# Four reorderings in a software-pipelined transformer-and-grid kernel: attention bias sum on GpSimd in slot 14, derivative sum ahead of a score, adapter copy ahead of a tanh, norm of x2 ahead of x4's scaling

## The chip, the core and the metric

One core of one Trainium2 chip runs the whole program. The metric is the device time of one execution in microseconds, the median of several. The engines are named as the profile names them: PE (TensorE matmul), PEld (its weight loads), DVE (VectorE), ACT (ScalarE), POOL (GpSimd) and SP (SyncE, which here only issues DMAs).

## What is computed

For each of 16 samples of 256 x 256 numbers, four stages follow each other. Cut to what matters here:

```python
# L0: adapter with a per-sample expert, then a norm
hidden = gelu(x @ down_W.T + down_b)
hidden = hidden @ expert_W[id].T + expert_b[id] + domain_emb[id]
x = layernorm(hidden @ up_W.T + up_b + x) * gamma + beta
# L1: adaptive norm, attention of 16 heads with a bias and a mask, feed-forward
x1 = _ln(x) * (1 + scale) + shift
scores = q @ k.T / 4 + attention_bias; scores = where(mask, -inf, scores)
x2 = x1 + (softmax(scores) @ v) @ Wo + bo
x3 = x2 + gelu2(_ln(x2) * g2 + beta2 @ W1 + b1) @ W2 + b2      # gelu2(u) = u*sigmoid(1.702u)
# L2: one of three small networks by the sample's kind, then a norm
x4 = x3 + net(x3);  f = layernorm(x4) * gamma + beta
# L3: finite differences on a grid
df = -(d/dx(A0 f) + d/dy(A1 f)) + 0.5 * (second differences of B f)
out = maximum(f + df * dt, 0)
```

## The kernel before

Everything is laid out by hand. A loop over **turns** t = -2 to 18 is unrolled; each turn has 16 **slots** s = 0 to 15, one for each attention head. In a turn six samples are at work at once, in six phases: G (sample t+2: the adapter of L0), F (t+1: norm, x1, and the projections q, k, v), X (t: the scores of its 16 heads, one a slot), B (t-1: end of attention, x2, its norm n3, first half of the feed-forward), T (t-2: second half of the feed-forward, x3, the small network, x4, its norm f, and the products of f with the grids), U (t-3: the derivatives and the output). Each engine has its own program, written slot by slot in a fixed order; semaphores tie them together, and an engine that waits for one lets everything behind it wait.

What matters around the change:

- **POOL** (lines 443 to 491) has in each turn, in this order: the reciprocal square root of the variance of y (`power`, L449), x3c = x3 + bc (L466, slot 4), x1res = x1 + bo (L472, slot 5), the mask of F (L475, slot 6), `power` for x4 (slot 7), `power` for x2 (slot 8), x2b = x2 + b2 (L484, slot 13), `power` for xa (slot 13) and bcf (L489, slot 15). x1res has two buffers, by the sample's parity. So the x1res of F may be written only when B, which uses the same buffer, has made its x2: that is the wait for `x2_ready`, which DVE sets in slot 8 (L894).
- **DVE** (lines 824 to 955): at the head of each slot the score's bias and row maximum (L826, two instructions for the two halves of the rows, "bias s" below). Behind it come, among others: w = derivative sum + t_e (L851, slot 4), x2 and its statistics (L894, L753 to L760, slot 8), scaling of x4 (`norm_scale`, L773), norm of x2 (`norm_apply`, L766, gives n3) and shift of x4 (`norm_shift`, L781, gives f) in slot 9, n3l (L905) in slot 10, the grid products of f (L810), the feed-forward's product (L922) in slots 12 to 15. In the profile's rows x4, x3, x2 and x1 are all printed as `x`, n3 and ctxN as `n`, and the grids' products t_a, t_b as `wb`, t_c as `x`.
- **ACT**: the exponentials (L526), most copies of turned scores (L512), in slots 11 to 14 the first feed-forward layer (L594) and its tanh (L599), and in slot 12 the adapter copy g1 (L602), which stands behind the tanh.
- **PE**: in slot 4 the turning of x1 into `front_bank` (L975), which first waits for `w_ready`, since w is read from that bank; in slot 5 the first layer of the small network (L1005, `back_bank<-ctxT,wb`), with weights that SP loads in each turn (`wb`, L402); in slot 10 the turning of n3 (L975, `attend_bank<-ident,n`); in slot 13 the adapter's last product (L1244), which waits for g1.
- **SP**: in slot 0 it loads a pair of bias tiles, for which it waits until DVE has done bias 15 of the turn before (L358), then issues 16 small DMAs that stack the second half of q and k for the scores (L371, L372), and in slot 1 the load of `wb` (L402).

Of the kernel before, what the change touches and what calls it, by code (L numbers as in the profile page):

```python
# [7 lines left out]
ALU = mybir.AluOpType  # L8
# [88 lines left out]
def build(nc, d):  # L97

    with ExitStack() as ctx:
# [325 lines left out]
        def _(e):  # L425
# [28 lines left out]
            def body(t):  # L454
                G, F, X, B, T, U = phases(t)
                for s in range(SLOTS):
# [6 lines left out]
                    if s == 4 and T:  # L463
                        e.wait_ge(ev["bcf_ready"], T.n)
                        e.wait_ge(ev["x3_turned"], T.n)
                        e.tensor_tensor(x3c[:, :, :], x3[:, :, :], rows(bcf[:, :]), ALU.add).then_inc(ev["x3c_ready"], 1)  # L466
                    if s == 5 and F:
                        wait(e, ev["x2_ready"], F.i - 1)
                        e.wait_ge(ev["x1_turned"], F.n)
                        if t == -1:  # L470
                            e.wait_ge(ready, 3 + SET0)
                        e.tensor_tensor(x1res[:, F.par, :, :], x1[:, :, :], rows(bo[:, :]), ALU.add).then_inc(ev["x1res_ready"], 1)  # L472
# [22 lines left out]
        def _(e):  # L495
# [18 lines left out]
            def body(t):  # L514
# [3 lines left out]
                for s in range(SLOTS):  # L518
# [71 lines left out]
                    if s in (11, 12, 13, 14) and B:  # L590
                        j = s - 11
                        quarter(e, "w1_done", B, j)
                        for m in range(2 * j, 2 * j + 2):
                            i = e.activation(ffT[:, m, :], two((bbank, abank)[j % 2])[:, m % 2, :], ACT.Identity, bias=b1c[:, m:m + 1])  # L594
                        i.then_inc(ev["u1_ready"], 1)
                        quarter(e, "u1_ready", B, j)
                        if j >= 2:
                            quarter(e, "ff_ready", B, j - 2)
                        e.activation(th[:, j % 2, :, :], ffT[:, 2 * j:2 * j + 2, :], ACT.Tanh, scale=0.851).then_inc(ev["th_ready"], 1)  # L599
                    if s == 12 and G:  # L600
                        e.wait_ge(ev["expert_done"], G.n)
                        e.activation(g1[:, :], fbank[:, 0:S], ACT.Identity, bias=wexp[:, A:A + 1]).then_inc(ev["g1_ready"], 1)  # L602

# [8 lines left out]
        def _(e):  # L612
# [199 lines left out]
            def body(t):  # L812
                G, F, X, B, T, U = phases(t)
                for s in range(SLOTS):
                    for t0, s0, setup in ((-2, 5, set_projections), (-1, 9, set_feed_forward), (0, 3, set_conditional),
                                          (0, 5, set_grids), (0, 8, set_edges)):
                        if is_step(t, s, t0, s0):
                            setup()
                    if X:
                        head(e, scored, X, s)  # L820
# [26 lines left out]
                    if s == 4 and U:  # L847
                        e.wait_ge(ev["d_done"], U.n)
                        e.wait_ge(ev["e_ready"], U.n)
                        e.wait_ge(ev["e_cols"], U.n)  # L850
                        e.tensor_tensor(t_e[:, :, :], two(fbank), t_e[:, :, :], ALU.add).then_inc(ev["w_ready"], 1)  # L851
                        e.wait_ge(ev["w_ready"], U.n)
                        e.scalar_tensor_tensor(out=t_e[:, :, :], in0=t_e[:, :, :], scalar=dt[:, bass.ds(U.i, 1)], in1=fN[:, :, :],
                                               op0=ALU.mult, op1=ALU.add).then_inc(ev["w2s_ready"], 1)
# [36 lines left out]
                    if s == 8 and B:  # L891
# [3 lines left out]
                        e.wait_ge(ev["x2_ready"], B.n)  # L895
                        norm_stats(B, 2, x2, ev["x2_stats"], ev["x2_aggr"], ev["x2_var"])
                    if s == 9 and T:
                        norm_scale(T, 3, x4, gamma3[:, :], ev["x4_rstd"], ev["f_scaled"])
                    if s == 9 and B:
                        norm_apply(B, 2, n3, x2, ev["x2_rstd"], ev["n3_ready"])  # L900
                    if s == 9 and T:
# [417 lines left out]
```

## Time and profile before

| | |
|---|---|
| median of 3 runs | 966.0 us (964.74 to 970.55) |
| the profiled execution | 969.76 us, of which the span of the trace is 967.6 us |
| mean granted PE clock over the span | 0.984 of full speed |
| PE busy | 853.4 us, 88% |
| PEld busy | 717.6 us, 74% |
| DVE busy | 730.9 us, 76% |
| ACT busy | 608.8 us, 63% |
| POOL busy | 164.1 us, 17% |
| DMA | 137.57 MB, mean 142 GB/s |

The span has three parts. Up to about 180 us the pipeline fills, from there to about 868 us each turn has the same work, and then it drains. A busy share is a mean over all three. In the timelines a row is one instruction, or several alike merged (x4), with its start, its length, and in square brackets the idle time of its engine just before it and what ended that. An instruction's start and length include the time in which it waits for a memory port.

### The profile page before, as it was taken

To read this page: it belongs to the slowest core of one execution; us is meant where nothing else is said; L and a number is where in the kernel's file an instruction comes from. 1 tells how busy PE (TensorE), PEld (TensorE's weight loads), DVE (VectorE), ACT (ScalarE), POOL (GpSimd) and SP (SyncE) were. 2 spreads that over 40 slices of the span, in tenths; PEclk is the share of its full clock that TensorE was granted. 3 is DMA by queue.
4 is the path that set the end of the run, shared out by engine and by line. 5 is a ranking of instruction groups with operands and counts; after the bars stand their busy time and mean duration, and the time that the engine had idled before them with its cause. 6 is when DMAs were issued, how large, how long until landed. Compare 5 with 4: busy or idle time off the path is not lost.

```text
span 967.6 us, 18458 instructions
## 1 busy us (share of the span) xinstructions
PE 853.4 (88%) x5962; PEld 717.6 (74%) x5962; DVE 730.9 (76%) x2441; ACT 608.8 (63%) x1247; POOL 164.1 (17%) x160
## 2 busy tenths in 40 slices
PE   2486789999999999999999999999999999898974
PEld 0274668788878878888888888887887888787773
DVE  3538676797878789696979787887979697859465
ACT  1113668786767676776868676767777686667420
POOL 2011002030211211210302112112102030211010
PEclk9997999999999999999999999999999999999988
DMA  6614365546453645555454635454544545362100
GB/s 205 199 50 128 129 184 170 153 140 175 135 175 104 180 138 162 156 159 161 141 174 153 165 118 160 138 167 151 168 153 148 170 145 165 108 172 91 47 26 22
DMA packets 147735, 137.57 MB, mean 142 GB/s; under 512 B 19298, under 2 KB 144803, under 8 KB 147636
## 3 DMA queue, kind: packets, MB, share of 16 engines
q1 hardware_dynamic: 147636, 136.33, 47.4%
q8 instruction: 53, 0.87, 0.4%
q14 instruction: 46, 0.38, 0.1%
HBM read 98.49 MB, written 4.23 MB: 106 GB/s over the span
## 4 chain that ended last, share of the span: by engine, by line
PE 57%; ACT 13%; DVE 13%; POOL 5%; SPq 5%; issue 5%; DMA 2%; POOLq 0%; DVEq 0%; ACTq 0%
PE back_bank L1034 10%; PE turn_bank L990 7%; PE front_bank L1059 5%; PE front_bank L1028 5%; PE context_bank L1044 5%; PE score_bank L1092 4%; PE score_bank L1093 4%; PE back_bank L1005 3%; PE back_bank L1014 3%; ACT sc L526 3%; PE attend_bank L1014 3%; PE attend_bank L1028 2%; ACT ffT L594 2%; POOL mask_neg L475 2%; SPq L306 2%
## 5 line engine op out<-in xcount | busy, mean ns | idle before, releaser
L826 DVE CUSTOM_DVE_ANT_0 sc<-score_bank,side 128x256 f32<-128x256 f32 x512 | 195.4, 419 | 92.3 <-PE score_bank L1093 84.7
L526 ACT ACTIVATE sc<-sc,negmax 128x256 f32<-128x256 f32 x512 | 230.0, 499 | 25.4 <-DVE negmax L826 24.9
L512 ACT ACTIVATE pt<-turn_bank 128x512 f32<-128x512 f32 x176 | 104.7, 595 | 176.0 <-PE turn_bank L990 144.8
L990 PE MATMUL turn_bank<-ident,sc 128*128 128x128 f32 x1024 | 157.9, 277 | 1.3 <-ACT sc L526 1.2
L990 PEld LDWEIGHTS turn_bank<-ident,sc 128*128 128x128 f32 x1024 | 124.7, 142 | 35.2 <-issue 14.0
L1092 PE MATMUL score_bank<-ks,qs 128*128 128x256 f32 x512 | 124.0, 324 | 6.7 <-DVE negmax L826 6.7
L1034 PE MATMUL back_bank<-w,ffT 128*128 128x256 f32 x512 | 118.0, 379 | 0.0
L1034 PEld LDWEIGHTS back_bank<-w,ffT 128*128 128x128 f32 x512 | 97.0, 190 | 12.6
L1093 PE MATMUL score_bank<-mask_neg,ident_r 128*128 128x512 f32 x256 | 103.0, 402 | 0.0
L1092 PEld LDWEIGHTS score_bank<-ks,qs 128*128 128x128 f32 x512 | 79.6, 195 | 15.3 <-DVE negmax L826 8.7
L449 POOL TENSOR_TENSOR rstd<-var,half_neg 128x2 f32<-128x2 f32 x64 | 49.5, 781 | 216.3 <-DVE var L760 215.0
L1044 PE MATMUL context_bank<-pt,vp 128*18 128x256 f32 x1024 | 68.6, 386 | 1.7 <-ACT pt L512 1.7
L472 POOL TENSOR_TENSOR x1res<-x,bo 128x512 f32<-128x512 f32 x16 | 20.6, 1290 | 273.3 <-DVE x L894 248.1
L955 DVE COPY pt<-turn_bank 128x512 f32<-128x512 f32 x80 | 54.7, 683 | 10.0 <-PE turn_bank L990 9.9
L484 POOL TENSOR_TENSOR x<-x,b2r 128x512 f32<-128x512 f32 x16 | 21.1, 1320 | 167.8 <-DVE xa L932 164.4
L1093 PEld LDWEIGHTS score_bank<-mask_neg,ident_r 128*128 128x128 f32 x256 | 49.2, 192 | 0.0
L922 DVE SCALAR_TENSOR_TENSOR ffT<-th,ffT 128x512 f32<-128x512 f32 x64 | 43.9, 686 | 4.0 <-ACT th L599 3.9
L1044 PEld LDWEIGHTS context_bank<-pt,vp 128*18 128x18 f32 x1024 | 24.1, 97 | 26.1 <-issue 10.3
L826 DVE DVE_READ_ACCUMULATOR2_ANT negmax<- 128x1 f32 x512 | 42.0, 82 | 0.0
L599 ACT ACTIVATE th<-ffT 128x512 f32<-128x512 f32 x64 | 40.5, 632 | 2.0
L1028 PE MATMUL back_bank<-n3h,w 128*128 128x256 f32 x128 | 36.7, 287 | 5.1 <-DVE n3l L905 5.1
L1059 PE MATMUL front_bank<-t_u,d1T 128*128 128x256 f32 x128 | 33.9, 388 | 8.3 <-DVE t_u L928 8.3
(199 smaller groups left out, 1935.5 us busy)
## 6 DMA issues: line engine op xcount, KB each, us to landing
side<-in_side SPq DMA_DIRECT2D x128, 512.0 KB, 5.0
qs<-qh SPq DMA_DIRECT2D x128, 64.0 KB, 2.6
ks<-kh SPq DMA_DIRECT2D x128, 64.0 KB, 2.6
ks<-kl SPq DMA_DIRECT2D x128, 64.0 KB, 2.6
qs<-ql SPq DMA_DIRECT2D x128, 64.0 KB, 2.6
wb<-in_wb SPq DMA_DIRECT2D x16, 512.0 KB, 3.9
xN<-in_x SPq DMA_DIRECT2D x16, 256.0 KB, 4.1
ada<-ada_rows SPq DMA_DIRECT2D x16, 256.0 KB, 5.3
```

The costliest lines, as they stand in the source:

```text
L512: e.activation(pt[:, h % NP2, :, :], two(tbank[h % 2]), ACT.Copy).then_inc(copied[h % 4], 1)
L526: i = e.activation(sc[:, h % NS, q, :], sc[:, h % NS, q, :], ACT.Exp, bias=negmax[:, q, h:h + 1], scale=-1.0)
L826: i = e.tensor_tensor_reduce(sc[:, s % NS, q, :], two(sbank[s % 2])[:, q, :], side[:, (H * X.i + s) % NSIDE, q, :], -1.0, 3.4e38, ALU.add, ...
L955: e.tensor_copy(pt[:, h % NP2, :, :], two(tbank[h % 2])).then_inc(copied[h % 4], 1)
L990: i = e.transpose(tbank[h % 2][:, k * S + q * P:k * S + q * P + P], sc[:, h % NS, q, k * P:k * P + P], ident[:, :])
L1014: i = e.matmul(two(dst)[:, q, :], xt[:, k, q * P:q * P + P], w[:, k, :], start=(k == 0), stop=(k == KT - 1))
L1028: i = e.matmul(two(dst)[:, m, :], a[:, k, c], b[:, k, :], start=(n == 0), stop=(n == 3 * KT - 1))
L1034: i = e.matmul(two(bbank)[:, q, :], ffT[:, k, q * P:q * P + P], w2[:, k, :], start=(q == 0 and k == 0), stop=(q == TT - 1 and k == FM - 1))
L1044: i = e.matmul(two(cbank)[CG * j:CG * j + VW, g % 2, :], vp[:, x.par, k, QD * g + j, :], pt[:, j, k, :], start=(k == 0), stop=(k == TT - 1))
L1059: i = e.matmul(two(fbank)[:, q, :], m[:, k, q * P:q * P + P], u[:, k, :], start=(n == 0 and k == 0), stop=(n == 1 and k == KT - 1))
L1092: e.matmul(two(sbank[s % 2])[:, q, :], qs[:, s // 2, q * P:q * P + P], ks[:, s, :], start=(q == 0), stop=False)
L1093: i = e.matmul(sbank[s % 2][:, :], ident_r[:, :], mask_neg[:, X.par, :, :], start=False, stop=True)
```

## The change

Four pieces of work stand elsewhere in their engines' programs. Nothing is added to the work and nothing is removed; one wait is exchanged for another.

- POOL: x1res = x1 + bo goes from slot 5 to slot 14, and waits for `x1_ready` and no more for `x1_turned`; the wait for `x2_ready` stays.
- ACT: the adapter copy g1 of slot 12 goes ahead of that slot's tanh.
- DVE: w of slot 4 goes ahead of bias 4, with its waits; the product with dt that uses it stays behind.
- DVE: in slot 9 `norm_apply` (n3) goes ahead of `norm_scale` (x4).

```diff
@@ POOL
-                    if s == 5 and F:
+                    if s == 14 and F:
                         wait(e, ev["x2_ready"], F.i - 1)
-                        e.wait_ge(ev["x1_turned"], F.n)
+                        e.wait_ge(ev["x1_ready"], F.n)
@@ ACT
+                    if s == 12 and G:
+                        e.wait_ge(ev["expert_done"], G.n)
+                        e.activation(g1[:, :], fbank[:, 0:S], ACT.Identity, bias=wexp[:, A:A + 1]).then_inc(ev["g1_ready"], 1)
+                    if s in (11, 12, 13, 14) and B:
+                        j = s - 11
                         quarter(e, "u1_ready", B, j)
...
                         e.activation(th[:, j % 2, :, :], ffT[:, 2 * j:2 * j + 2, :], ACT.Tanh, scale=0.851).then_inc(ev["th_ready"], 1)
-                    if s == 12 and G:
-                        e.wait_ge(ev["expert_done"], G.n)
-                        e.activation(g1[:, :], fbank[:, 0:S], ACT.Identity, bias=wexp[:, A:A + 1]).then_inc(ev["g1_ready"], 1)
@@ DVE
+                    if s == 4 and U:
+                        e.wait_ge(ev["d_done"], U.n)
+                        e.wait_ge(ev["e_ready"], U.n)
+                        e.wait_ge(ev["e_cols"], U.n)
+                        e.tensor_tensor(t_e[:, :, :], two(fbank), t_e[:, :, :], ALU.add).then_inc(ev["w_ready"], 1)
                     if X:
                         head(e, scored, X, s)
...
                     if s == 4 and U:
-                        e.wait_ge(ev["d_done"], U.n)
-                        e.wait_ge(ev["e_ready"], U.n)
-                        e.wait_ge(ev["e_cols"], U.n)
-                        e.tensor_tensor(t_e[:, :, :], two(fbank), t_e[:, :, :], ALU.add).then_inc(ev["w_ready"], 1)
                         e.wait_ge(ev["w_ready"], U.n)
...
+                    if s == 9 and B:
+                        norm_apply(B, 2, n3, x2, ev["x2_rstd"], ev["n3_ready"])
                     if s == 9 and T:
                         norm_scale(T, 3, x4, gamma3[:, :], ev["x4_rstd"], ev["f_scaled"])
-                    if s == 9 and B:
-                        norm_apply(B, 2, n3, x2, ev["x2_rstd"], ev["n3_ready"])
```

POOL's program over one turn, from slot 4 to slot 15, in the kernel before:

```order
L466 TENSOR_TENSOR x<-x,bcr 128x512
L472 TENSOR_TENSOR x1res<-x,bo 128x512
L475 TENSOR_SCALAR mask_neg<-mask_raw 128x512
L449 TENSOR_TENSOR rstd<-var,half_neg 128x2 x2
L484 TENSOR_TENSOR x<-x,b2r 128x512
L449 TENSOR_TENSOR rstd<-var,half_neg 128x2
L489 TENSOR_SCALAR bcr<-bcr,flags 128x256
```

and in the changed kernel:

```order
L466 TENSOR_TENSOR x<-x,bcr 128x512
L475 TENSOR_SCALAR mask_neg<-mask_raw 128x512
L449 TENSOR_TENSOR rstd<-var,half_neg 128x2 x2
L484 TENSOR_TENSOR x<-x,b2r 128x512
L449 TENSOR_TENSOR rstd<-var,half_neg 128x2
L472 TENSOR_TENSOR x1res<-x,bo 128x512
L489 TENSOR_SCALAR bcr<-bcr,flags 128x256
```

The sum x1res has left its place ahead of the mask and of the two `power` instructions of x4 and x2, and stands now between the `power` of xa and bcf (printed as bcr).

DVE's program in slot 9 before, from bias 9 to bias 10:

```order
L826 ISA sc,negmax<-score_bank,side 128x256
L826 ISA negmax 128x1
L773 SCALAR_TENSOR_TENSOR x<-x,mv,gamma 128x256 x2
L766 TENSOR_SCALAR n<-x,mv,rstd 128x256 x2
L781 SCALAR_TENSOR_TENSOR fN<-x,rstd,beta 128x256 x2
```

and in the changed kernel, whose lines lie two or more further down (L833 is the bias, L768 the norm of x2, L775 the scaling, L783 the shift):

```order
L833 ISA sc,negmax<-score_bank,side 128x256
L833 ISA negmax 128x1
L768 TENSOR_SCALAR n<-x,mv,rstd 128x256 x2
L775 SCALAR_TENSOR_TENSOR x<-x,mv,gamma 128x256 x2
L783 SCALAR_TENSOR_TENSOR fN<-x,rstd,beta 128x256 x2
```

The norm of x2 has changed places with the scaling of x4; the shift stays third.

## Rows read from the trace of the kernel before

**Rows 1.** Busy time by engine of the even part: busy us (instructions), clock, DMA share
```profile
180.00:868.00 688.00, 654.37 (x4792) 559.63 (x4792) 557.19 (x1853) 490.52 (x1006) 127.18 (x115) 1.00 0.52 153
```
**Rows 2.** Who waited for whom: us in total, times, longest us
```profile
PE attend_bank L975 <- DVE n L766: 20.0, 16, 4.0
PE front_bank L975 <- DVE t_e L851: 8.3, 12, 0.7
PE front_bank L1244 <- ACT g L602: 6.9, 15, 0.6
```
**Rows 3.** Timeline of POOL: start us, length us, engine, line, operation
```profile
460.29 1.29 POOL L472 TENSOR_TENSOR x1res<-x,bo 128x512 f32<-128x512 f32 x1 [17.69 <-DVE x L894]
461.55 1.50 POOL L475 TENSOR_SCALAR mask_neg<-mask_raw 128x512 fp32r<-128x512 uint8 x1
463.01 1.38 POOL L449 TENSOR_TENSOR rstd<-var,half_neg 128x2 f32<-128x2 f32 x2
```
**Rows 4.** Timeline of DVE, slots 8 to 9 of the same turn
```profile
461.31 0.29 DVE L760 TENSOR_SCALAR var<-mv 128x2 f32<-128x2 f32 x1
461.84 0.42 DVE L826 CUSTOM_DVE_ANT_0 sc<-score_bank,side 128x256 f32<-128x256 f32 x1 [0.24 <-PE score_bank L1093]
463.77 0.88 DVE L773 SCALAR_TENSOR_TENSOR x<-x,mv,gamma 128x256 f32<-128x256 f32 x2 [1.15 <-POOL rstd L449]
```
**Rows 5.** Timeline of PE, slot 10
```profile
463.15 1.06 PE L1044 MATMUL context_bank<-pt,vp 128*18 128x256 f32 x16
465.36 0.66 PE L975 MATMUL attend_bank<-ident,n 128*128 128x128 f32 x4 [1.15 <-DVE n L766]
```
**Rows 6.** Timeline of SP, slots 0 and 1 of the next turn
```profile
482.67 0.37 SPq L358 DMA_DIRECT2D side<-in_side  x1
...
494.40 0.41 SPq L402 DMA_DIRECT2D wb<-in_wb  x1
```
**Rows 7.** Timelines of SP and PE: load of wb and its first use, three turns
```profile
441.91 0.40 SPq L402 DMA_DIRECT2D wb<-in_wb  x1
446.48 1.97 PE L1005 MATMUL back_bank<-ctxT,wb 128*128 128x256 f32 x8
...
499.26 1.03 PE L1005 MATMUL back_bank<-ctxT,wb 128*128 128x256 f32 x4
...
653.05 0.40 SPq L402 DMA_DIRECT2D wb<-in_wb  x1
658.33 1.03 PE L1005 MATMUL back_bank<-ctxT,wb 128*128 128x256 f32 x4
```
**Rows 8.** Timeline of DVE, slots 14 and 15
```profile
479.59 0.68 DVE L922 SCALAR_TENSOR_TENSOR ffT<-th,ffT 128x512 f32<-128x512 f32 x1
480.20 0.88 DVE L810 TENSOR_TENSOR x<-fN,grid_c 128x512 f32<-128x512 f32 x1
482.21 0.42 DVE L826 CUSTOM_DVE_ANT_0 sc<-score_bank,side 128x256 f32<-128x256 f32 x1
```
**Rows 9.** Timelines of POOL in slot 15 and of ACT in slot 12
```profile
479.54 1.45 POOL L489 TENSOR_SCALAR bcr<-bcr,flags 128x256 f32<-128x256 f32 x1
...
474.22 0.46 ACT L602 ACTIVATE g<-front_bank,wexp 128x256 f32<-128x256 f32 x1
```
**Rows 10.** Timelines of DVE and POOL, slots 9 to 10 at the drain's start; L781's lengths, min/median/max ns
```profile
882.58 1.90 DVE L781 SCALAR_TENSOR_TENSOR fN<-x,rstd,beta 128x256 f32<-128x256 f32 x2
882.75 1.46 POOL L484 TENSOR_TENSOR x<-x,b2r 128x512 f32<-128x512 f32 x1 [1.51 <-DVE n L766]
L781 DVE SCALAR_TENSOR_TENSOR fN<-x,rstd,beta x32: 475/478/1510, 199.5 to 953.3; 128x256 f32<-128x256 f32 x32
```
**Rows 11.** Timeline of DVE and PE, slots 9 to 11 of the last sample
```profile
920.63 0.87 DVE L773 SCALAR_TENSOR_TENSOR x<-x,mv,gamma 128x256 f32<-128x256 f32 x2
921.69 0.73 DVE L766 TENSOR_SCALAR n<-x,mv,rstd 128x256 f32<-128x256 f32 x2 [0.19 <-POOL rstd L449]
924.98 0.55 PE L1028 MATMUL back_bank<-n3h,w 128*128 128x256 f32 x1 [1.84 <-DVE n3l L905]
```

## The prediction

> **What bounds the kernel now.** The busy time of the even part comes first: PE works 654.4 of 688 us and the clock is full, DVE 557.2 [rows 1]. So PE is nearly serial, and what an edit can win is idle time of PE, 33.6 us in 13 turns. The waits say where that lies [rows 2]: 20.0 us before the turning of n3 (16 times), 8.3 us before the turning of x1 behind w (12 times, none over 0.7), 6.9 us before the adapter's product behind g1 (15 times). These are the three waits that the four edits are aimed at.
>
> The timeline shows what makes the first. In slot 8 POOL waits for x2, then does x1res, the mask and both `power` instructions in a row, from 460.29 to 464.39 [rows 3]. DVE has done the variance of x2 at 461.60, and after bias 9 it stands idle for 1.15 us up to 463.77 [rows 4], because the first `power`, that of x4, is behind x1res and the mask. PE stands idle for 1.15 us before 465.36 for the n3 that comes out of it [rows 5].
>
> Then one has to ask whether PE alone carries the turn. From 463.77 on DVE has no gap up to bias 15, whose second half starts at 482.21 and ends at 482.63 [rows 4, 8]. SP waits for just that: its bias load starts at 482.67, the 16 stacking DMAs follow, and the load of wb is issued at 494.40 [rows 6]. PE uses wb for the first time at 499.26 [rows 7]. In the turn before, issue and first use are 4.57 us apart (441.91, 446.48), here 4.86, and 5.28 in a third (653.05, 658.33) [rows 7]. The shortest of these is what the transfer and its signal take: PE waited for wb there. Over 13 turns, eight have this short distance (up to 5.0 where the transfer took longer) and five are 0.3 to 0.7 us longer. So there are two loops of nearly one length, PE's own work, and **DVE's slots 9 to 15, then SP's 16 DMAs, then wb, then PE's slots 5 to 9**. The second has a slack of 5 x about 0.6 = 3.1 us over all turns, and that is all that PE can win before it waits for wb instead.
>
> **The change part by part.** The sum is made against the profiled 969.76 us (span 967.6); the median of the three runs is 966.0, 3.8 lower.
>
> (a) POOL's order, with n3 ahead of the scaling. `power` for x4 now runs in slot 7. That for x2 starts right behind its variance, 461.6, and takes 0.69 (half of 1.38) [rows 3], done at 462.3, before bias 9 ends at 462.6. DVE goes on at once: its 1.15 us are gone, and so are PE's [rows 4, 5]. With n3 first, it is ready at 462.6 + 0.73 = 463.35 (0.73 is the norm's length [rows 11]), while PE is busy with the context product up to 464.2 (463.15 + 1.06) [rows 5]. The old order behind the early `power` would give n3 at about 464.15, also in time, so the swap costs and wins nothing here; its cover is that context product, and without it would be worth one scaling, 0.88. DVE's loop: **-1.15** a turn.
>
> (b) x1res in slot 14. It is queued behind the `power` of xa, in bcf's old place, which starts at 479.54 [rows 9]; x1res starts there now, and bcf behind it. DVE at that time has two products of two SBUF tensors each, the feed-forward's at 479.59 and t_c at 480.20 [rows 8]. What such a pair does to each other the drain shows: x2b, a sum of the same shape as x1res, starts at 882.75 within the first half of the shift of x4; the two halves together take 1.90 us, and the longest half of this line is 1510 ns where the median is 478 [rows 10]. So POOL's sum stops DVE's for **1.03** us. The variance shows the same: started at 461.31, it ends at 461.60, as soon as x1res does (460.29 + 1.29) [rows 3, 4]. At 479.59 the feed-forward's product isn't slowed by bcf, which takes 1.45, but t_c is, 0.88 against 0.68 for its neighbours; that 0.2 is there before and after. So x1res waits through the first product, gets in between the two, and t_c ends 1.03 later. Bounds: nothing, if it fell beside the one-input biases; 1.25, if it started first and its whole 1.29 were waited for. I take 1.03, the row of the same pair. This is ahead of bias 15, in the stretch without gaps, so it goes in full into the DVE loop: **+1.03**. Behind x1res wait bcf, which x3c needs only in slot 4 of the next turn, some 12 us later, and `power` of y, 8 us later; neither is late.
>
> The Trainium skill, page "SBUF — State Buffer", section "Who interferes with whom", has a rule that speaks against this edit: a VectorE instruction with two SBUF inputs and a GpSimd instruction that reads SBUF exclude each other, and the second to issue waits for the whole of the first. The trace agrees. By the rule alone DVE would lose x1res's whole 1.29 instead of 1.03, and the DVE loop would be 0.1 us longer than now and not shorter.
>
> (c) w ahead of bias 4. The derivative products are done before the scores of slot 4, and DVE waits for these anyway, so bias 4 isn't late, and PE's 0.69 goes [rows 2]. But the next thing on PE is wb in slot 5, and it waits there instead: nothing, or up to the slack. If bias 4 did wait it would be for w's 0.69.
>
> (d) g1 ahead of the tanh. PE's 0.43 (6.9 / 15) goes [rows 2]; the tanh is later by the copy's 0.46 [rows 9], and its user on DVE, the feed-forward's product of slot 13, stands behind other work of an engine without gaps, so it hides; without that cover it would be 0.46. It too only feeds the slack.
>
> (e) Ends. In the filling part POOL's x1res no longer meets DVE's set-up work, and turn 1 has part of the waits: -0.4, between -1.5 and +0.5. In the drain it costs: for the last sample DVE scales x4 at 920.63, while `power` of x2 still runs, and PE waits 1.84 us at 924.98 for n3l, which is behind all three norm steps [rows 11]. With n3 first, the scaling (0.87) comes behind 921.69 and delays n3l: +0.7, nothing hides it.
>
> Sum: 13 x (-1.15 + 1.03) = -1.6; slack used by PE, which (a), (c) and (d) give it many times over, -3.1; ends +0.3. That is **-4.4**, 965.4 for the profiled execution and, with 3.8 off, **962 us** for the median.
>
> **The rivals.**
>
> *POOL's sum doesn't stop DVE in slot 14* (it falls beside the biases, or shares). Then the DVE loop is 1.15 shorter: 13 x 1.15 + 3.1 - 0.3 = 17.7, 948 us. For it: bcf left the feed-forward's product alone, and the statistics under x1res are not slowed today. Against: three halves at about 1.5 us, and two products back to back just where x1res starts. 13%.
>
> *wb doesn't hold PE* (its waits are short because PE is late, and SP moves with PE). Then PE's waits all go, 13 x (1.15 + 0.69 + 0.43) = 29.5, or 937 us, if x1res is hidden too. Against: SP starts on DVE's bias 15 and nothing of PE's. 3%.
>
> *The other side: both POOL instructions stop DVE.* x1res holds up one product for 1.03 to 1.29 and bcf, pushed behind it, the next for up to its 1.45. Then a turn gains 1.15 and loses 2.5, 13 x 1.35 - 3.1 + 0.3 = +14.7: 981 us. It makes the kernel slower by 1% from 2.1 us a turn on. Against: bcf costs 0.2 today beside the same kind of product. 5%.
>
> *The edits do nothing measurable*: the block is 1.25 and the slack is eaten by longer transfers, 966 to 968. I count it in the forecast's own range.
>
> **How the numbers follow.** The forecast has 79%. Its own range: block 0.83 to 1.25 (964.8 at the upper end, 959.4 at the lower), slack 1 to 4, ends 1 to either side, and the runs of before spread by 5.8: 957 to 968. Ahead of it lie 16% (948 and 937), behind it 5%. To leave out no more than 2 in 10 the range goes from 954 to 968. Within 1% of 966.0 (956.3 to 975.7, about what a measurement here can tell from no change) lies nearly all of the forecast: 0.78. Faster by over 1%: 16% and a little of its lower tail, 0.17. Slower by over 1%: 0.05.
>
> **What the profile after would show.** (a) right: no idle time of DVE before the norm of x2 in slot 9, and the row of PE waiting for n3 down from 20.0 to about 5, from the two turns at the end. (b) right: in slot 14 either t_c or the feed-forward's product takes 1.5 to 1.9 us, and bias 9 to the end of bias 15 takes about 20.7 us, nearly as now (461.84 to 482.63, 20.8); wrong: all near 0.68. (c), (d): the waits for w and g1 are gone from the list, and PE's idle time before L1005 has grown to 1.5 to 2.2 us in every turn. (e): n3l of the last sample comes later against its x2. The prediction falls if L1005 starts later than 5 us after the issue of wb in most turns, for then wb isn't the bound, or if DVE's two products are as long as before.

## The result, and the profile after

| | before | changed |
|---|---|---|
| median | 966.7 us (964.7 to 970.6, 4 runs) | 979.7 us (976.2 to 983.3, 4 runs) |
| profiled execution, its span | 969.76 us, 967.6 us | 977.65 us, 975.7 us |
| fill, up to the first use of `wb` in turn 2 | 180.7 us | 172.5 us |
| even part, 13 turns from one first use of `wb` to the next | 687.5 us | 700.8 us |
| drain | 99.4 us | 102.3 us |

The ratio is 1.013 (95% interval 1.0076 to 1.0183). The change makes the kernel slower by 1.3%; the forecast was 962 us and "within 1%". 979.7 us also lies beyond the range, which ended at 968.

The fill must be read with care. A second profiled execution of each kernel (`before_again`, `after_again`, below) had fills of 176.5 and 176.1 us, but even parts of 691.3 and 703.0 and drains of 99.8 and 102.0. So the even part is longer by 11.7 to 13.3 us in both pairs and the drain by 2.2 to 2.9, while the fill's gain of 8.2 us in the first pair is not there in the second.

This is the even part in windows, first of the kernel before, then of the changed one. The columns are: stretch, its length, busy us (instructions) of PE, PEld, DVE, ACT, POOL, then PE's granted clock, the DMA share and GB/s.

```profile
181.00:868.00 687.00, 654.09 (x4792) 559.34 (x4790) 556.34 (x1851) 489.53 (x1005) 127.18 (x115) 1.00 0.52 153
```

```profile
172.00:873.00 701.00, 665.87 (x4790) 571.49 (x4791) 568.96 (x1852) 489.24 (x1003) 130.56 (x114) 0.98 0.52 150
```

PE has the same work (4790 instructions), yet is busy 11.8 us longer, and its granted clock is 0.98 where it was 1.00. DVE is busy 12.6 us longer, about 0.97 a turn. The waits of PE show where idle time went (us in total, times, longest):

```profile
PE back_bank L1008 <- DMA wb<-in_wb: 30.5, 13, 3.3
PE attend_bank L978 <- DVE n L768: 3.8, 1, 3.8
```

The waits for n3, w and g1 of [rows 2] are gone, but for one in the drain, and in their place stands one wait a turn for `wb`, before the product of slot 5 (L1008 here, L1005 before). That wait is 1.4 to 3.3 us long. Twelve of the 13 lie between the first and the last of the starts that bound the even part, 28.2 us together; the same sum was 2.4 us before. PE's rows around two of them, in neighbouring turns:

```profile
387.64 3.75 PE L1008 MATMUL back_bank<-ctxT,wb 128*128 128x256 f32 x8 [3.16 <-DMA wb<-in_wb]
```

```profile
442.86 1.97 PE L1008 MATMUL back_bank<-ctxT,wb 128*128 128x256 f32 x8 [1.87 <-DMA wb<-in_wb]
```

The same eight matmuls take 3.75 us behind a wait of 3.16 and 1.97 us behind a wait of 1.87. The windows ahead of, behind and well behind the first of them tell why (columns as above):

```profile
377.00:387.00 10.00, 7.48 (x60) 5.86 (x58) 7.41 (x27) 7.07 (x14) 2.74 (x2) 0.98 0.46 137
387.60:394.40 6.80, 6.76 (x26) 5.91 (x27) 1.30 (x4) 2.94 (x5) 0.00 (x0) 0.58 0.80 236
394.40:403.50 9.10, 9.10 (x72) 7.72 (x71) 6.66 (x26) 4.55 (x11) 0.72 (x1) 1.00 0.24 59
```

In the 6.8 us behind the wait PE is busy throughout, gets 26 instructions done and has a granted clock of 0.58. The kernel before did 56 in the same 6.8 us of the turn, at a clock of 1.00:

```profile
393.50:400.30 6.80, 6.76 (x56) 5.65 (x57) 5.27 (x21) 6.50 (x12) 0.00 (x0) 1.00 0.77 240
```

The lower stretches are PE at the 1.2 GHz level instead of 2.4 GHz. The 13 turns can be cut at two instructions, the product of slot 5 and bias 9 on DVE, which has to wait for PE's scores. In the kernel before, each turn takes 15.3 to 15.4 us from the one to the other. In the changed one six turns take 15.4, five 16.9 to 17.1, and two 18.2 and 18.3. In every one of the seven long ones the clock records show the lower clock, from between 1.1 us before the product starts to 0.9 us after it, for 3.4 us, or for 6.8 us in the longest two. So the turn is put together as follows (sums over 13 turns, us):

| stretch of a turn | before | changed | difference |
|---|---|---|---|
| product of slot 5 to bias 9 | 199.4 | 213.6 | +14.2 |
| bias 9 to the end of bias 15 (DVE; before, with its 1.15 us of idle time in slot 9) | 269.1 | 268.7 | -0.4 |
| end of bias 15 to the next product of slot 5 (SP, transfer, PE) | 219.0 | 218.6 | -0.4 |

In the second pair of traces the three differences are +14.7, -0.6 and -2.4. So the even part got longer in the one stretch in which PE loses time at half clock, and in no other.

The clock records of the changed kernel have one more drop in the even part, in its last turn, where some phases have run out of samples. PE waits 2.76 us there for n3l in slot 11, which was 1.64 before, and runs at the lower clock for 3.4 us behind it, in both traces. It hardly counts here (that turn's bias 9 to bias 15 takes 19.80 us, 19.57 before), but it comes again in `wb_first` and in the drain.

### The profile page after: what moved, and what is told of

Its sections match the earlier page's. It is cut to its first block, busy times and chain, and to the rows that moved or that the text cites. A ratio compares the mean times of both kernels' runs of the same rounds, so it can differ in the third digit from the quotient of the medians.

```text
span 975.7 us, 18459 instructions
## 1 busy us (share of the span) xinstructions
PE 859.2 (88%) x5962; PEld 725.2 (74%) x5962; DVE 741.7 (76%) x2441; ACT 608.5 (62%) x1247; POOL 168.5 (17%) x160
## 4 chain that ended last, share of the span: by engine, by line
PE 33%; DVE 29%; SPq 17%; issue 10%; DMA 7%; ACT 3%; POOL 1%; DVEq 0%; POOLq 0%
SPq L371 7%; SPq L372 6%; DVE sc L833 6%; DMA wb<-in_wb 5%; PE front_bank L1031 4%; PE turn_bank L993 4%; PE back_bank L1008 4%; DVE ffT L925 3%; PE back_bank L1017 3%; PE attend_bank L1017 2%; PE front_bank L1201 2%; DVE pt L958 2%; PE context_bank L1047 2%; PE back_bank L1037 2%; SPq L306 2%
## 5 line engine op out<-in xcount | busy, mean ns | idle before, releaser
L833 DVE CUSTOM_DVE_ANT_0 sc<-score_bank,side 128x256 f32<-128x256 f32 x512 | 195.3, 419 | 56.0 <-PE score_bank L1096 48.2
L993 PE MATMUL turn_bank<-ident,sc 128*128 128x128 f32 x1024 | 160.9, 281 | 1.6 <-ACT sc L526 1.5
L993 PEld LDWEIGHTS turn_bank<-ident,sc 128*128 128x128 f32 x1024 | 127.2, 144 | 36.4 <-issue 14.7
L1037 PEld LDWEIGHTS back_bank<-w,ffT 128*128 128x128 f32 x512 | 97.1, 190 | 12.6
L1008 PE MATMUL back_bank<-ctxT,wb 128*128 128x256 f32 x128 | 41.6, 482 | 30.5 <-DMA wb<-in_wb 30.5
L925 DVE SCALAR_TENSOR_TENSOR ffT<-th,ffT 128x512 f32<-128x512 f32 x64 | 56.7, 885 | 3.5 <-ACT th L604 3.5
L1008 PEld LDWEIGHTS back_bank<-ctxT,wb 128*128 128x128 f32 x128 | 29.4, 240 | 39.2 <-issue 34.3
L1047 PEld LDWEIGHTS context_bank<-pt,vp 128*18 128x18 f32 x1024 | 24.8, 97 | 29.5 <-issue 15.7
L833 DVE DVE_READ_ACCUMULATOR2_ANT negmax<- 128x1 f32 x512 | 42.0, 82 | 0.0
```

The costliest lines, as they stand in the source:

```text
L833: i = e.tensor_tensor_reduce(sc[:, s % NS, q, :], two(sbank[s % 2])[:, q, :], side[:, (H * X.i + s) % NSIDE, q, :], -1.0, 3.4e38, ALU.add, ...
L925: e.scalar_tensor_tensor(out=f, in0=th[:, j % 2, :, :], scalar=1.0, in1=f, op0=ALU.add, op1=ALU.mult).then_inc(ev["ff_ready"], 1)
L993: i = e.transpose(tbank[h % 2][:, k * S + q * P:k * S + q * P + P], sc[:, h % NS, q, k * P:k * P + P], ident[:, :])
L1008: i = e.matmul(two(dst)[:, m, :], w[:, k, c0 + m * P:c0 + m * P + P], xt[:, k, :], start=(k == 0), stop=(k == n_k - 1))
L1037: i = e.matmul(two(bbank)[:, q, :], ffT[:, k, q * P:q * P + P], w2[:, k, :], start=(q == 0 and k == 0), stop=(q == TT - 1 and k == FM - 1))
L1047: i = e.matmul(two(cbank)[CG * j:CG * j + VW, g % 2, :], vp[:, x.par, k, QD * g + j, :], pt[:, j, k, :], start=(k == 0), stop=(k == TT - 1))
```

## The experiments

`after` is the changed kernel. Each run is compared with the kernel before on the same chip.

### The clock, apart from the waiting: fill_pe and fill_pe4

In `after`, eight dummy products go into the place of the wait, so that PE works instead of standing idle. They write to the bank that the following product overwrites.

```diff
                         if T:
                             e.wait_ge(ev["x3T_ready"], T.n)
+                            for n in range(8):
+                                e.matmul(two(bbank)[:, n % 2, :], ident[:, :], x3T[:, n % KT, :], start=True, stop=True)
                             e.wait_ge(ld_kind, times(T, 32))
```

> The changed kernel, with eight extra matmuls of 128x256 in each turn on PE in slot 5, between the turning of x1 and the wait for wb; they write the bank that the small network's first layer overwrites, so nothing that is computed changes. In the changed kernel PE is idle for 1.4 to 3.3 us before L1008, and in 7 of 13 turns its granted clock is 0.5 in the stretch after that, which makes the stretch from L1008 to bias 9 1.5 to 3.0 us longer (13.9 us in all). Theory 'idle, then clock': the eight matmuls take 1.9 us of this idle time, cost nothing where the wait is longer than that, and the clock stays at 1.0 in the even part: 8 to 14 us less than the changed kernel's 980, so 964 to 972. Theory 'more work': the loss comes from DVE and SP (x1res in slot 14) and the clock is a by-product; then the extra matmuls win nothing or cost their own 1.9 us a turn where they stick out: 980 or more.

Measured: 982.3 us, ratio 1.0174 (1.0157 to 1.0191); even part 699.4 us.

```profile
493.13 3.62 PE L1149 MATMUL back_bank<-ctxT,ident 128*128 128x256 f32 x16
496.58 1.89 PE L1008 MATMUL back_bank<-ctxT,wb 128*128 128x256 f32 x8
174.00:873.00 699.00, 692.71 (x5000) 598.88 (x4999) 570.53 (x1859) 490.65 (x1007) 130.72 (x114) 1.00 0.52 151
```

The dose was mis-sized. Eight calls in fp32 are 16 rows of the trace, and the product of slot 5 starts 3.45 us later for them (493.13 to 496.58), not 1.9. That is longer than nearly all the waits it was to fill, so PE never waits for `wb` and becomes the serial bound: ten turns take 53.78 us and three up to 53.89, and 13 x 53.78 = 699.1. So the 964 to 972 us that were expected were missed, and the time alone would fit the rival's "980 or more"; it is the trace that tells them apart. The clock stayed at 1.00 through the even part, with every stretch up to bias 9 at 15.3 to 15.4 us, and 3.45 us of added work a turn cost nothing against `after` in the even part (699.4 to 700.8). For a clean answer the same was done with four calls.

> The changed kernel with four extra matmul calls in slot 5 ahead of the wait for wb, where fill_pe had eight. In fill_pe's trace the eight calls are 16 rows and take 3.45 us (493.13 to 496.58), more than the wait, so that each turn is PE's own 53.78 us; but no turn of the even part had the clock at 0.5, and the stretch from the use of wb to bias 9 was 15.3 us in all 13 turns, where the changed kernel has up to 18.3. Four calls take 1.73 us and leave 0 to 1.5 us of the wait. Theory 'idle, then clock': the clock stays up in all or nearly all turns, the turn is the wb loop again, 52.7 to 53.2 us, and the even part is 685 to 692 us, not 701: 962 to 972 in all. Theory 'chance': the clock falls as often as in the changed kernel, and the time is 976 to 983.

Measured: 971.1 us, ratio 1.0039 (1.0016 to 1.0062); even part 685.1 us.

```profile
173.00:858.00 685.00, 673.00 (x4897) 578.57 (x4897) 570.14 (x1859) 490.02 (x1008) 131.17 (x114) 1.00 0.54 154
PE back_bank L1008 <- DMA wb<-in_wb: 4.9, 6, 1.4
L1008 PE MATMUL back_bank<-ctxT,wb x128: 379/379/483, 172.8 to 939.6; 128*128 128x256 f32 x128
```

The same line of `after` (shortest, median and longest ns of one):

```profile
L1008 PE MATMUL back_bank<-ctxT,wb x128: 379/380/767, 172.5 to 952.4; 128*128 128x256 f32 x128
```

The only difference to `after` is 1.73 us of useless work a turn, 20.8 us in the twelve turns with a wait. PE's idle time ahead of the product goes from 28.2 to 5.6 us, by 22.6, so it is nearly this work alone that fills it. But no matmul of the product is longer than 483 ns (767 in `after`), all 13 stretches up to bias 9 take 15.3 to 15.4 us, and the even part is 15.7 us shorter, of which the half clock of the table above is 14.2. In the traces this shows the cause of the loss in the even part. By the medians the kernel gets 8.6 us faster by working more (979.7 to 971.1, on two chips on which the kernel before takes 966.7 and 967.4).

The traced execution is the fastest of ten (964.0 to 975.1 us), 7 us below their median. Whether the clock also stayed up in the nine others no trace shows; a fill that differs by up to 8 us from trace to trace could make as much.

### How often a wait lowers the clock: before_again and after_again

Both kernels unchanged, for a second trace each.

> The kernel before, unchanged, for a second trace. The changed kernel's trace reaches the first use of wb after 172.5 us, that of before after 180.7, and ten traces of ten kernels lie from 172.5 to 180.7. If most of this is the PE clock in the first 60 us, which differs from one execution to the next, this trace reaches it after 174 to 181, and set-up and projection matmuls differ in length with it. If it is the edits, it is 180 to 181 again.

> The changed kernel, unchanged, for a second trace. 'Idle, then clock' says that the clock falls again in the even part, in 5 to 9 of 13 turns and not in the same ones, always just behind a wait for wb of over 1.5 us; even part 696 to 706 us. A bound by DVE or SP alone would give the same turn lengths as the first trace.

Measured: 969.7 and 983.1 us. In `before_again` one turn of 13 is long, behind the one wait of 2.66 us; in `after_again` nine are (waits of 1.99 to 4.0 us). The even part of `after_again`:

```profile
176.00:879.00 703.00, 668.08 (x4792) 573.01 (x4793) 568.44 (x1851) 489.18 (x1004) 131.20 (x114) 0.97 0.53 150
PE back_bank L1008 <- DMA wb<-in_wb: 30.8, 13, 4.0
```

The 13 turns of eight traces (the two of before, the two of after, and pool_alone, no_pool, fill_pe4, x1res_late) give 104 waits ahead of that product, each with its stretch up to bias 9. Every stretch is either 15.3 to 15.4 us or 16.8 to 18.3 (long):

| PE idle ahead of the product of slot 5 | turns | of these long |
|---|---|---|
| under 0.5 us | 30 | 0 |
| 0.5 to 1.0 | 17 | 0 |
| 1.0 to 1.5 | 15 | 3 |
| 1.5 to 2.0 | 14 | 3 |
| 2.0 to 2.5 | 14 | 10 |
| over 2.5 | 14 | 12 |

Between 1.0 and 2.9 us waits of about one length go either way. What decides for one of them is not settled here. The length of the wait alone doesn't: in `before`, `before_again` and `before_wb_first` PE waits 1.13 to 1.27 us for n3 in each of the 39 turns, and the clock falls behind none of these.

The wait for n3l in the last turn goes both ways too. At 2.75 to 2.76 us the clock fell behind it in `after`, `after_again` and `wb_first` and not in `fill_pe` and `fill_pe4`, at 1.86 in `x1res_late` and not in `both`, and at 1.63 to 1.64 in none of five traces.

### The POOL edit alone and left out: pool_alone and no_pool

`pool_alone` is the kernel before with x1res in slot 14 and nothing else:

```diff
-                    if s == 5 and F:
+                    if s == 14 and F:
                         wait(e, ev["x2_ready"], F.i - 1)
-                        e.wait_ge(ev["x1_turned"], F.n)
+                        e.wait_ge(ev["x1_ready"], F.n)
```

`no_pool` is the opposite: the changed kernel with x1res back in slot 5, so it has the swap of slot 9 and the moves of w and g1.

> The kernel before with the move of x1res to slot 14 alone; w, g1 and the order of slot 9 as before. Theory 'idle, then clock': PE is earlier by 1.15 us a turn and not by 2.3, the DVE loop is as long as before, so PE waits 0.6 to 2 us for wb, and the clock falls in fewer turns, 0 to 3: 962 to 972. Theory 'x1res blocks DVE': the move alone makes the whole loss: 976 to 983.

> The changed kernel with x1res back in slot 5, so w ahead of bias 4, g1 ahead of the tanh and n3 ahead of the scaling, without the POOL move. Theory 'idle, then clock': PE is earlier by 0.69 + 0.43 us a turn, which it then waits for wb (1.0 to 1.5 us), and the clock falls in few turns or none: 962 to 970. Theory 'x1res blocks DVE': no loss without it, so it is as fast as before or faster, 960 to 967. The two differ in pool_alone and fill_pe; this one tells what the three small edits are worth by themselves.

Measured: `pool_alone` 968.2 us, ratio 0.9993 (0.9961 to 1.0024); `no_pool` 982.0 us, 1.0175 (1.0153 to 1.0196). Even parts 692.9 and 701.2. Their windows and PE's waits, `pool_alone` first:

```profile
177.00:870.00 693.00, 664.17 (x4792) 566.50 (x4792) 567.09 (x1851) 491.04 (x1005) 130.65 (x114) 0.99 0.53 152
PE back_bank L1005 <- DMA wb<-in_wb: 14.6, 10, 3.1
PE attend_bank L975 <- DVE n L766: 4.7, 2, 4.0
```

```profile
175.00:877.00 702.00, 658.14 (x4794) 563.10 (x4795) 559.41 (x1857) 493.44 (x1006) 126.57 (x115) 0.99 0.52 150
PE back_bank L1008 <- DMA wb<-in_wb: 21.1, 13, 2.5
465.97 0.74 DVE L768 TENSOR_SCALAR n<-x,mv,rstd 128x256 f32<-128x256 f32 x2 [1.81 <-POOL rstd L449]
```

x1res in slot 14 alone takes the n3 wait away (20.0 to 4.7) and makes bias 9 to bias 15 shorter by 3.1 us in all (266.0 against 269.1). PE then waits 13.1 us for `wb` in the even part, and five turns are long. Gain and loss meet: no difference that can be measured. The time lies in the range that was expected, the five long turns do not (0 to 3). The traced execution is the slowest of ten (958.9 to 972.2 us), so the others may have had fewer.

In `no_pool` the swap of slot 9 costs. With both `power` instructions still late on POOL, DVE has nothing to do while n3 waits for the second; its idle time is 1.81 us where it was 1.15 [rows 4], and bias 9 to bias 15 takes 21.5 us a turn instead of 20.7 (279.4 over 13). With three long turns on top, the three edits without the POOL move are slower by 1.75%. Both theories had expected this kernel at 970 us or less; neither had the swap's price in it, 10.3 us over the 13 turns (279.4 against 269.1), which is more than the three long turns cost (+5.4 up to bias 9).

### The late transfer itself: wb_first and before_wb_first

SP issues the load of `wb` ahead of the 16 stacking DMAs of slot 0, not behind them. Once on `after`, once on the kernel before.

```diff
-                    if s == 0 and X:
-                        stack(X, B, 1)
-                    if s == 1 and T:
+                    if s == 0 and T:
                         kind = e.value_load(ids_ok[0:1, 2, bass.ds(T.i, 1)], min_val=0, max_val=NC2 - 1)
                         wait(e, ev["e_ready"], T.p)
                         e.dma_start(wb[:, :, :], ...).then_inc(ld_kind, 16)
+                    if s == 0 and X:
+                        stack(X, B, 1)
```

> The changed kernel with SP's load of wb ahead of the 16 stacking DMAs of slot 0, not behind them. If the wait for wb is what holds PE (as forecast, and shown in the trace by the issue-to-use distance of 4.5 us in 12 of 13 turns), PE no longer waits at L1008, each turn is PE's own serial work, about 50.5 us, the clock stays up, and 13 x (54 - 50.5) = 45 us go: 930 to 945. If DVE's stretch from slot 9 to 15, with x1res's block in it, is a bound of its own by another way than wb, the turn stays at 52 to 53: 960 or more.

> The kernel before with SP's load of wb ahead of the stacking DMAs, nothing else. wb_first took 14 us idle time and 49 us in all from the changed kernel. If before has only about 3 us of waits for wb in its 13 even turns, the load's place is worth 2 to 5 us here: 960 to 966, and the four edits are then worth 30 us (931.6 against this), since PE's waits of 1.15, 0.69 and 0.43 us a turn are all that is left between 52.7 and 50.3 us a turn. If wb first were worth 30 us or more by itself, the four edits would be worth nothing in any case.

Measured: `wb_first` 931.6 us, ratio 0.964 (0.9623 to 0.9656), even part 657.0; `before_wb_first` 958.2 us, 0.9899 (0.9867 to 0.993), even part 683.1. SP's and PE's rows of one turn of `wb_first`, and the windows of both:

```profile
411.16 0.39 SPq L400 DMA_DIRECT2D wb<-in_wb  x1
411.60 0.58 SPq L371 DMA_DIRECT2D qs<-qh  x1
424.06 1.89 PE L1008 MATMUL back_bank<-ctxT,wb 128*128 128x256 f32 x8
173.00:829.00 656.00, 649.69 (x4789) 561.43 (x4788) 568.38 (x1858) 487.01 (x1007) 131.30 (x115) 0.99 0.57 161
```

```profile
176.00:859.00 683.00, 652.27 (x4794) 559.67 (x4792) 557.42 (x1860) 490.71 (x1009) 126.52 (x115) 1.00 0.55 154
```

The load is issued 12.9 us ahead of its use and not under 5, PE has no idle time before the product, and it works 649.7 of 656 us: 12 turns take 50.31 us each, PE's own length. The 13th takes 53.2, and the reason is the wait for n3l again (PE's row, then the window of the lower clock, columns as above):

```profile
798.03 0.55 PE L1031 MATMUL back_bank<-n3h,w 128*128 128x256 f32 x1 [2.75 <-DVE n3l L908]
797.30:804.20 6.90, 6.17 (x28) 6.11 (x29) 6.70 (x19) 3.18 (x7) 0.00 (x0) 0.51 0.49 151
```

`before_wb_first` came out 2 us below its expectation. Here the four edits are worth what they take from PE: 958.2 to 931.6, 26.6 us, and 26.1 by the even parts. The same four edits that cost 13 us with `wb` late bring 27 us with `wb` early.

### The block in slot 14: x1res_late, both, both_scale_first

`x1res_late` is `after` with x1res in slot 1 of the next turn, where DVE has no product of two SBUF tensors:

```diff
+                    if s == 1 and X:
+                        wait(e, ev["x2_ready"], X.i - 1)
+                        e.wait_ge(ev["x1_ready"], X.n)
+                        if F:
+                            e.wait_ge(ev["y_ready"], F.n)
...
+                        e.tensor_tensor(x1res[:, X.par, :, :], x1[:, :, :], rows(bo[:, :]), ALU.add).then_inc(ev["x1res_ready"], 1)
                     if s == 1 and F:
                         power(F, 1, ev["y_var"], ev["y_rstd"])
...
-                    if s == 14 and F:
...
-                        e.tensor_tensor(x1res[:, F.par, :, :], x1[:, :, :], rows(bo[:, :]), ALU.add).then_inc(ev["x1res_ready"], 1)
```

`both` joins it with `wb` first, and `both_scale_first` puts slot 9 back into the old order (scaling of x4, then norm of x2).

> The changed kernel with x1res not in slot 14 but in slot 1 of the next turn, behind the norm y, where DVE does one-input statistics and then waits for PE. Forecast's reading: x1res in slot 14 stops DVE's two-input products for 1.0 to 1.1 us in the loop DVE - SP - wb. Then here bias 9 to bias 15 takes 19.3 us, not 20.4 (13.5 us less in 13 turns), PE waits 1 us less for wb, so the clock falls in fewer turns, 0 to 3: 948 to 960. If x1res doesn't stop DVE, or DVE is held by something else, nothing changes: 976 to 983.

> wb_first with x1res in slot 1 of the next turn. Once wb is there in time, PE's own 50.31 us make the turn, and x1res's 1.1 us on DVE lie in time that DVE has left: as wb_first, 929 to 933. If DVE's block in slot 14 held PE by another way too, 2 to 14 us less.

> The kernel 'both' (wb first, x1res late) with slot 9 in the old order: scaling of x4, then the norm of x2. In the even part n3 is then ready at about the moment PE comes to it (464.15 against 464.21 in before's times, as the forecast has it), so the turn stays 50.3 us. In the drain the norm of the last sample no longer pushes the scaling behind the power: 1 to 2 us less there (both: 102.3 us of drain, before 99.4). 928 to 931 in all. Rival: n3 comes too late for PE by some 0.1 to 0.9 us a turn, and the kernel is 1 to 10 us slower than both.

Measured: `x1res_late` 957.5 us, ratio 0.9882 (0.9839 to 0.9925), even part 679.1; `both` 930.3 us, 0.9617 (0.958 to 0.9654), drain 102.3; `both_scale_first` 929.2 us, 0.9586 (0.956 to 0.9611), drain 99.3. The window and the feed-forward's product (busy us, mean ns) in `x1res_late`, and the window of `both_scale_first`:

```profile
179.00:858.00 679.00, 657.54 (x4792) 564.55 (x4792) 556.28 (x1852) 487.80 (x1004) 125.60 (x114) 0.99 0.53 155
L927 DVE SCALAR_TENSOR_TENSOR ffT<-th,ffT 128x512 f32<-128x512 f32 x64 | 44.0, 687 | 3.5 <-ACT th L606 3.5
```

```profile
174.00:827.00 653.00, 647.13 (x4793) 560.19 (x4792) 554.36 (x1863) 487.32 (x1008) 126.37 (x115) 1.00 0.57 161
```

In `x1res_late` DVE's busy time is back at 556.3 (568.96 in `after`), the product's mean is 687 ns, and bias 9 to bias 15 is 13.0 us shorter than in `after` (255.7 against 268.7): x1res in slot 14 costs DVE 1.0 us a turn. Three turns of 13 are still long, in the slowest of its four executions. With `wb` early DVE's loop bounds nothing: the first 12 turns take 50.3 us in `both` as in `wb_first`, and the intervals of the two overlap. The even part of `both` is 3.5 us shorter (653.5), all of it in the last turn, where the clock didn't fall. The old order of slot 9 gives the drain its 3.0 us back, against 1 to 2 expected. `both_scale_first`, the fastest, is 4.1% faster than the kernel before.

## Why the prediction was wrong

**The two loops: right.** DVE's slots 9 to 15, SP's DMAs and `wb` were the second loop, and PE waited for `wb` in every turn once its other waits were gone, 1.4 to 3.3 us where 1.5 to 2.2 had been named. `wb_first` shows the loop as the cause: the wait goes with the order on SP.

**(a), POOL's order: right, in mechanism and size.** The `power` for x2 now starts right behind its variance, and DVE goes from bias 9 into the norm with no idle time:

```profile
457.94 0.69 POOL L449 TENSOR_TENSOR rstd<-var,half_neg 128x2 f32<-128x2 f32 x1 [3.29 <-DVE var L762]
458.57 0.42 DVE L833 CUSTOM_DVE_ANT_0 sc<-score_bank,side 128x256 f32<-128x256 f32 x1
458.92 0.73 DVE L768 TENSOR_SCALAR n<-x,mv,rstd 128x256 f32<-128x256 f32 x2
```

The 1.15 us of idle time that DVE had there [rows 4] are gone, as forecast. "The swap costs and wins nothing" held only in the first 12 turns of the even part and only together with the POOL move: `no_pool` shows +0.8 us a turn without it, and the swap makes PE wait longer for n3l in the last one.

**(b), x1res against DVE: right in size, off in place.** In slots 14 and 15 (POOL's two rows first, then DVE's):

```profile
474.77 1.28 POOL L472 TENSOR_TENSOR x1res<-x,bo 128x512 f32<-128x512 f32 x1
476.02 1.89 POOL L489 TENSOR_SCALAR bcr<-bcr,flags 128x256 f32<-128x256 f32 x1
474.85 1.75 DVE L925 SCALAR_TENSOR_TENSOR ffT<-th,ffT 128x512 f32<-128x512 f32 x1
476.52 0.68 DVE L812 TENSOR_TENSOR x<-fN,grid_c 128x512 f32<-128x512 f32 x1
477.12 0.36 DVE L806 TENSOR_TENSOR edge_t<-fN,edge_e 128x16 f32<-128x16 f32 x1
```

x1res did not wait through the feed-forward's product. It started 0.08 us ahead of it and held it up: 1.75 us against 0.68 [rows 8], +1.07. t_c got shorter, 0.68 against 0.88, and edge_t took 0.36 instead of 0.16 beside bcf. The net of the three is +1.07; the term said +1.03. For the case that x1res started first, which is what happened, the forecast had 1.25 as its bound; the product lost 1.07 of the 1.20 us that x1res still had to run. The Trainium skill, page "SBUF — State Buffer", section "Who interferes with whom", says that issue order decides who blocks. The trace agrees: x1res was in front, and the product was held up; bcf was issued while that product ran, and was itself drawn out to 1.89 us (1.45 in [rows 9]). But which instruction starts first in the profile doesn't tell it in every case: in the kernel before, bcf starts 0.05 us ahead of the same product, which is not held up (0.68), while t_c behind it is (0.88) [rows 8, 9]. Over a turn the DVE stretch changed by -0.03 us (-0.4 / 13), where the sum had -0.12. `x1res_late` confirms the price: 1.0 us a turn comes back when the sum is moved away.

**(c) and (d), w and g1: the step that failed.** (The 0.43 us of g1 should be 0.46 by the division beside it, 6.9 / 15; nothing hangs on it.) The waits for w and g1 are gone and PE "waits there instead", as said. The error is in the words behind it, "nothing, or up to the slack": an idle microsecond was priced at one microsecond wherever it lies. The kernel before had three short waits a turn, of about 1.15, 0.69 and 0.4 us, and its clock stayed at 1.00. The changed one has about the same idle time in one piece (28.2 us in twelve, 2.35 on average), and behind that piece PE ran at the 1.2 GHz level in 7 of 13 turns (9 in the second trace), 1.5 to 3.0 us lost each time. That term stood at zero and measured +14.2 us. The trace of `fill_pe4` shows it by itself: with work in place of the idle time the loss is gone, while `wb` comes as late as before.

**The slack of 3.1 us: mis-sized.** PE was to win it. The stretch from the end of bias 15 to the product of slot 5, in which SP's queue and the transfer lie, got only 0.4 us shorter in all, and 2.4 in the second pair of traces. In the first pair SP took 0.8 us more for the stacking DMAs over the 13 turns, and the transfers of `wb` landed 1.3 us later after their issue; these differ from trace to trace by as much as the slack itself (SP 2.0 us less in the second pair).

**(e), the ends.** The drain was forecast at +0.7 and measured +2.2 to +2.9. The last sample is as forecast:

```profile
928.49 0.73 DVE L768 TENSOR_SCALAR n<-x,mv,rstd 128x256 f32<-128x256 f32 x2 [0.81 <-POOL rstd L449]
929.14 1.89 DVE L775 SCALAR_TENSOR_TENSOR x<-x,mv,gamma 128x256 f32<-128x256 f32 x2
932.79 0.55 PE L1031 MATMUL back_bank<-n3h,w 128*128 128x256 f32 x1 [2.39 <-DVE n3l L908]
```

The scaling, put behind the norm, is now itself held up by POOL's x2b, 1.89 us against 0.87 [rows 11], and the idle time ahead of the norm is 0.81 instead of 0.19. From the end of x2 to PE's first product with n3 it takes 6.37 us, 5.53 before: +0.84. What was left out lies one sample earlier. There the same swap makes PE wait 2.55 us for n3l, which was 1.63 before, and behind that wait the clock falls for 3.4 us:

```profile
891.33 0.36 PE L1031 MATMUL back_bank<-n3h,w 128*128 128x256 f32 x1 [2.55 <-DVE n3l L908]
891.70:895.10 3.40, 3.40 (x18) 3.40 (x18) 3.37 (x12) 1.11 (x3) 1.32 (x1) 0.50 0.00 0
```

From this sample's turn to the next, product of slot 5 to product of slot 5, `after` takes 44.0 us and the kernel before 42.2. That is +1.8, of which most is the clock: in `no_pool`, where PE waits the same 2.55 us and the clock doesn't fall behind it, it takes 42.4. In `both_scale_first`, which has the old order, PE waits 1.64 us there, the clock doesn't fall, and the drain goes from 102.3 to 99.3. For the fill -0.4 was forecast. It ranges from 172.5 to 180.7 us over all the traces, both extremes in the first pair, and differs by 0.4 in the second pair, so what the edits do there stays open. PE's clock, which was suspected, doesn't explain it: it was low for 17.1 us of the longest fill (`before`) and for 40.9 us of the shortest (`wb_first`).

**The sum, as measured in the first pair of traces:** +14.2 for the clock, -0.4 for DVE, -0.4 for the rest, +2.9 in the drain, -8.2 in the fill, 8.1 us in span. The medians stand 13.0 us apart, which agrees with +11.7 to +13.3 in the even part, +2.2 to +2.9 in the drain, and a fill that favours neither by much. Of the rivals none was it: the one on the other side reached 981 us, but by POOL stopping two products of DVE, and DVE's stretch didn't get longer.

**What stays open:** why a wait of, say, 2.2 us lowers the clock in one turn and not in the next; why the lower clock lasts 3.4 us in most turns and 6.8 in some; how often it falls in the executions that were not traced; and the edits' part in the fill.

## What to carry to other kernels

Before you take short waits away from PE, look for the transfer or the engine that it will wait for next, and ask how long the single wait becomes in which the short ones gather; here three waits of 0.4 to 1.15 us cost their own length, and one of 2 us or more mostly cost 1.5 to 3 us on top, in slower matmuls behind it. Compare PE's busy time for the same number of instructions and the granted clock of a stretch, since the list of waits does not show this loss. And mend the late transfer first: the four edits cost 13 us behind a late `wb` and bring 27 us behind an early one, for which one DMA moved ahead of 16 others in a queue.

## What was unexpected of the hardware

PE's granted clock fell behind single waits of 1.0 to 4.0 us in a program that otherwise keeps PE busy 95% of the time: never in 47 turns with under 1 us, in 6 of 29 between 1 and 2, in 22 of 28 above 2 (waits ahead of the product of slot 5, eight traces). A turn in which it fell there was 1.4 to 3.0 us longer. Behind the 39 waits of 1.13 to 1.27 us for n3 it never fell.

A POOL sum of 1.27 to 1.29 us held up the same one of DVE's products in 12 turns of each of the six traces in which it stood in slot 14, by 1.06 to 1.08 us: the product started 0.08 us behind it and took 1.74 to 1.76 us, where it takes 0.68 without it.
